# Residual written into product banks by ScalarE, and half of the low parts on VectorE, in two convolution stages

## The reference

```python
# layer 2
out = conv3x3(gn(x), w3 * m3) + einsum('oi,bihw->bohw', w1 * (~m3), gn(x)) + b.sum(axis=1)
x = x + out
# layer 3
g = gn(x)
t = relu(bn(conv3x3(g, w1), ...1))
x = x + relu(bn(conv3x3(t, w2), ...2) + g)
```

## Time and profile before

| what | value |
|---|---|
| median of 3 runs | 3720.85 us (3720.38 to 3724.54) |
| time of the profiled execution | 3722.6 us |
| its span, first to last instruction | 3720.8 us |
| mean granted TensorE clock | 0.977 of full |
| PE busy | 3507.0 us, 94% of the span |
| DVE busy | 2367.6 us, 64% |
| ACT busy | 2116.1 us, 57% |
| POOL busy | 1666.0 us, 45% |

### The profile page before, as it was taken

One profiled execution on the slowest core, in us unless ns is written; L12 is line 12 of the kernel. 1 busy time (PEld: TensorE's weight loads), 2 busy tenths in 40 slices (PEclk: granted clock), 3 DMA queues, 4 the chain that ended last, 5 costly groups with the idle time before them and its releaser, 6 DMA issues. The chain is left out here.

```text
span 3720.8 us, 102442 instructions
## 1 busy us (share of the span) xinstructions
PE 3507.0 (94%) x31974; PEld 2970.3 (80%) x31974; DVE 2367.6 (64%) x6299; ACT 2116.1 (57%) x5882; POOL 1666.0 (45%) x2591
## 2 busy tenths in 40 slices
PE   7999899999999999969999999999999969979999
PEld 4656565656565665569999999999999969979998
DVE  5868787878778787833333333343333359988898
ACT  4979797979788787834443333333333324345554
POOL 2746464646465565600013333333334436556665
PEclk9999999999999999989999999999999979989999
DMA  6232323333232314111110000000002100000000
GB/s 222 69 101 74 99 77 93 83 94 82 85 90 66 101 58 118 48 73 45 51 40 0 0 0 0 0 0 0 0 17 62 62 16 1 1 31 18 35 35 35
DMA packets 202834, 193.93 MB, mean 52 GB/s; under 512 B 35745, under 2 KB 191137, under 8 KB 199457
## 3 DMA queue, kind: packets, MB, share of 16 engines
q1 hardware_dynamic: 171168, 177.15, 15.3%
q10 hardware_dynamic: 31360, 12.87, 1.3%
HBM read 123.30 MB, written 66.58 MB: 51 GB/s over the span
## 5 line engine op out<-in xcount | busy, mean ns | idle before, releaser
L197 PE MATMUL bank<-h,w_hh 128*128 128x128 f32 x8032 | 933.8, 275 | 0.0
L197 PEld LDWEIGHTS bank<-h,w_hh 128*128 128x128 f32 x8032 | 917.0, 192 | 0.0
L242 ACT ACTIVATE h<-bank,bg 128x128 f32<-128x128 f32 x1008 | 370.4, 367 | 818.2 <-PE bank L197 818.1
L1611 ACT ACTIVATE Pr<-bank,nmx 128x256 f32<-128x256 f32 x1568 | 724.0, 479 | 96.5 <-DVE nmx L1749 81.8
L1541 POOL TENSOR_TENSOR Pr<-Pr,rden 128x768 f32<-128x768 f32 x392 | 575.8, 1469 | 379.8 <-DVE rden L1828 379.8
L1749 DVE TENSOR_REDUCE nmx<-bank 128x1 f32<-128x256 f32 x1568 | 555.5, 416 | 173.6 <-PE bank L1955 167.8
L288 DVE SCALAR_TENSOR_TENSOR inp<-bank,b_in,tz 128x256 f32<-128x256 f32 x196 | 85.8, 479 | 696.3 <-ACT tz L225 696.3
L1966 PE MATMUL bank<-ident,Pr 128*128 128x128 f32 x3136 | 463.2, 285 | 17.4 <-POOL Pr L1541 14.8
L1966 PEld LDWEIGHTS bank<-ident,Pr 128*128 128x128 f32 x3136 | 335.4, 142 | 136.2 <-POOL Pr L1541 68.6
L1533 POOL COPY kg<-kT 128x64 f32 x1568 | 309.1, 244 | 296.2 <-DMA row<-ix 276.8
L1620 ACT ACTIVATE PT<-bank 128x512 f32<-128x512 f32 x784 | 427.3, 602 | 24.4 <-PE bank L1966 21.9
(11 more groups left out here) (263 smaller groups left out, 6480.6 us busy)
## 6 DMA issues: line engine op xcount, KB each, us to landing
v_rows<-v_padded SPq DMA_DIRECT2D x168, 232.0 KB, 3.3
vg<-v_windows SPq DMA_DIRECT2D x1176, 32.0 KB, 2.1
first_gates<-gate_sums SPq DMA_DIRECT2D x28, 512.0 KB, 2.6
gate_sums<-first_gates SPq DMA_DIRECT2D x28, 512.0 KB, 3.6
v_padded<-vpad SPq DMA_DIRECT2D x56, 232.0 KB, 2.1
X<-in_x SPq DMA_DIRECT2D x8, 1568.0 KB, 15.6
vg<-v_windows ACTq DMA_DIRECT2D x392, 32.0 KB, 2.2
x_backup<-X SPq DMA_DIRECT2D x8, 1568.0 KB, 6.0
```

What stands on the lines that cost most here:

```text
L197: ins = pe.matmul(bank[m][:, tt * COLS:(tt + 1) * COLS], w_hh[:, k, m * 128:(m + 1) * 128], prev[:, k, :], start=False, stop=(k == NH - 1) ...
L242: act.activation(h[:, 2 * q + tt, m, :], bank[m][:, tt * COLS:(tt + 1) * COLS], ACT.Tanh, bias=bg[:, 0, m:m + 1]).then_inc(s_h, 1)
L1611: act.activation(Pr[:, par, j, :], bank[j][:, 0:KEYS], ACT.Exp, bias=nmx[:, par, j:j + 1], accum_out=den[:, par, j:j + 1])\
```

## The change

In both stages:

- The residual goes into PSUM ahead of the products. A new ACT step `residual(q+1)` writes what is to be added to even columns into the bank of p0, and the negative of what is to be added to odd columns into the bank of p3 (two instructions of 128x392, function Identity with a bias; in the pair, for `i` = 1 only, also with a scale). The matmuls of these two banks (`held`) add onto it: their first one no longer starts a new sum.
- The outputs of every block are the four instructions that the pair's first convolution has already: ACT copies p1 (`first(q)`), DVE forms e = p2 + o, o = o - p2, e = e + p0, and later o = o - p3. L828, L829, L832 and L834 of the masked convolution become two, as do L1076, L1077, L1080 and L1082 of the pair. The pair's L999 (128x784 on ACT) is gone.
- The low part of the first half stays on POOL. That of the second half moves to DVE as `rest_lo(q)`, one instruction of 128x896 with both inputs in SBUF. In DVE's order it stands behind `outputs(q-2)`; in the masked convolution `part_stats(q-3)` follows it.

Once: PE runs four 128x512 float32 matmuls into banks 0, 3, 4 and 7 ahead of the masked convolution, DVE forms the negatives `nbsum`, `nA` and `ntb`, and the blocks 0 and 1 of each stage get their `rest_lo` ahead of the loop.

```diff
-def split_product(pe, ps, w, x, first, last):
+def split_product(pe, ps, w, x, first, last, held=False):
-    pe.matmul(ps, w[0], x[0], start=first, stop=False)
+    pe.matmul(ps, w[0], x[0], start=first, stop=False, skip_group_check=held)
...
                 def lo(q):
-                    for h in range(2):
-                        pool.wait_ge(s_hi, 2 * q + h + 1)
-                        pool.tensor_tensor(halves(v[:, q % 3, 1], h), halves(pts, h),
-                                           halves(v[:, q % 3, 0], h).bitcast(F32), ALU.subtract).then_inc(s_lo, 1)
+                    pool.wait_ge(s_hi, 2 * q + 1)
+                    pool.tensor_tensor(halves(v[:, q % 3, 1], 0), halves(pts, 0),
+                                       halves(v[:, q % 3, 0], 0).bitcast(F32), ALU.subtract).then_inc(s_lo, 1)
...
+                def residual(q):
+                    x = xrows(q).rearrange("p (k e) -> p k e", e=2)
+                    if q >= 2:
+                        act.wait_ge(s_e, 4 * (q - 1))
+                    act.activation(bank[4 * (q % 2)][:, 0:PROD], x[:, :, 0], ACT.Identity, bias=bsum[:]).then_inc(s_res, 1)
+                    act.activation(bank[4 * (q % 2) + 3][:, 0:PROD], x[:, :, 1], ACT.Identity, bias=nbsum[:], scale=-1.0)\
+                        .then_inc(s_res, 1)
+
+                def first(q):
+                    act.wait_ge(s_res, 2 * q + 2)
+                    act.wait_ge(s_m, 4 * q + 1)
+                    act.activation(xrows(q).rearrange("p (k e) -> p k e", e=2)[:, :, 1],
+                                   bank[4 * (q % 2) + 1][:, 0:PROD], ACT.Copy).then_inc(s_s1, 1)
...
                 for q in range(NQ):
                     n, b = divmod(q, NRB)
+                    first(q)
+                    if q + 1 < NQ:
+                        residual(q + 1)
                     if q + 2 < NQ:
                         hi(q + 2)
...
+                def rest_lo(q):
+                    dve.wait_ge(s_hi, 2 * q + 2)
+                    dve.tensor_tensor(halves(v[:, q % 3, 1], 1), halves(pts, 1),
+                                      halves(v[:, q % 3, 0], 1).bitcast(F32), ALU.subtract).then_inc(s_lor, 1)
+
                 def outputs(q):
-                    dve.wait_ge(s_m, 4 * q + 1)
-                    dve.scalar_tensor_tensor(o_, ps[1], bsum[:], o_, ALU.add, ALU.add).then_inc(s_e, 1)
-                    dve.scalar_tensor_tensor(e, ps[1], bsum[:], e, ALU.add, ALU.add).then_inc(s_e, 1)
+                    dve.wait_ge(s_s1, q + 1)
                     dve.wait_ge(s_m, 4 * q + 2)
-                    dve.wait_ge(s_e, 6 * q + 1)
+                    dve.tensor_tensor(e, ps[2], o_, ALU.add).then_inc(s_e, 1)
                     dve.scalar_tensor_tensor(o_, ps[2], -1.0, o_, ALU.mult, ALU.add).then_inc(s_e, 1)
-                    dve.wait_ge(s_e, 6 * q + 2)
-                    dve.tensor_tensor(e, ps[2], e, ALU.add).then_inc(s_e, 1)
...
                     if q + 2 < NQ:
                         points(q + 2)
                     outputs(q)
+                    if q + 2 < NQ:
+                        rest_lo(q + 2)
                     if q:
                         part_stats(q - 1)
...
+                pe.wait_ge(s_gd, GN_DVE + 5)
+                for j in (0, 3, 4, 7):
+                    pe.matmul(bank[j][:], group4[:], X[:, 0:512], start=True, stop=True).then_inc(s_own, 1)
                 pe.wait_ge(s_u, SPLIT_STEPS)
                 for q in range(NQ):
-                    pe.wait_ge(s_lo, 2 * q + 2)
+                    pe.wait_ge(s_lo, q + 1)
+                    pe.wait_ge(s_lor, q + 1)
                     if q >= 2:
-                        pe.wait_ge(s_e, 6 * (q - 1))
+                        pe.wait_ge(s_e, 4 * (q - 1))
                     for j in ORDER:
+                        held = j in (0, 3)
+                        if held:
+                            pe.wait_ge(s_res, 2 * q + (1 if j == 0 else 2))
```

More of the change, by code:

```diff
@@ L657, in _ @@
                         again_tensor(pe, r * PM + PA, r * PM + PM, r * PM + PM, r * 3 + 9)
-def split_product(pe, ps, w, x, first, last):
-    pe.matmul(ps, w[0], x[0], start=first, stop=False)
-    pe.matmul(ps, w[0], x[1], start=False, stop=False)
-    return pe.matmul(ps, w[1], x[0], start=False, stop=last)
+def split_product(pe, ps, w, x, first, last, held=False):
+    pe.matmul(ps, w[0], x[0], start=first, stop=False, skip_group_check=held)
+    pe.matmul(ps, w[0], x[1], start=False, stop=False, skip_group_check=held)
+    return pe.matmul(ps, w[1], x[0], start=False, stop=last, skip_group_check=held)
 BORDERS = 4
@@ L721, in masked_conv @@
         b2 = sb("b2", [C, C])
-        bsum = sb("bsum", [C, 1])
+        bsum, nbsum = sb("bsum", [C, 1]), sb("minus_bsum", [C, 1])
         u_hi, u_lo = sb("u_hi", [C, 12, C], F32R), sb("u_lo", [C, 12, C], F32R)
@@ L787, in _ @@
                 hi(1)
+                act.wait_ge(s_wr, 5)
+                act.wait_ge(s_own, 4)
+                residual(0)
                 for q in range(NQ):
                     n, b = divmod(q, NRB)
+                    first(q)
+                    if q + 1 < NQ:
+                        residual(q + 1)
                     if q + 2 < NQ:
@@ L803, in _ @@
                 dve.tensor_reduce(bsum[:], b2[:], AXX, ALU.add).then_inc(s_wr, 1)
-                dve.wait_ge(s_wr, 3)
+                dve.wait_ge(s_wr, 4)
+                dve.tensor_scalar(nbsum[:], bsum[:], -1.0, None, ALU.mult).then_inc(s_wr, 1)
                 def points(q):
@@ L857, in _ @@
                 points(0)
+                rest_lo(0)
                 points(1)
+                rest_lo(1)
                 for q in range(NQ):
@@ L882, in _ @@
                             ins = split_product(pe, bank[4 * (q % 2) + j][:, 0:PROD], (u_hi[:, k, :], u_lo[:, k, :]),
-                                                (v[:, q % 3, 0, SLOT[j], at], v[:, q % 3, 1, SLOT[j], at]), dy == 0, dy == 2)
+                                                (v[:, q % 3, 0, SLOT[j], at], v[:, q % 3, 1, SLOT[j], at]),
+                                                dy == 0 and not held, dy == 2, held)
                         ins.then_inc(s_m, 1)
@@ L928, in formed @@
         def formed(q):
-            n, i, b = block_of(q)
-            return n * 10 * NRB + (4 * NRB + 6 * b if i else 4 * b)
+            return 4 * q
         def halves(t, h):
@@ L996, in first, with residual @@
                         act.wait_ge(s_f, nth(q - 2) + 1)
+                    act.wait_ge(s_m, 4 * q + 1)
+                    act.activation(yp[q % 2][:, :, 1], bank[4 * (q % 2) + 1][:, 0:PROD], ACT.Copy).then_inc(s_s1, 1)
+                def residual(q):
                     n, i, b = block_of(q)
                     if i:
[L999 to L1003, removed]
+                        x = xrows(n, b).rearrange("p (k e) -> p k e", e=2)
+                        act.wait_ge(s_e, formed(q - 1))
+                        act.activation(bank[4 * (q % 2)][:, 0:PROD], x[:, :, 0], ACT.Identity,
+                                       bias=tb[:, n:n + 1], scale=A[:, n:n + 1]).then_inc(s_res, 1)
+                        act.activation(bank[4 * (q % 2) + 3][:, 0:PROD], x[:, :, 1], ACT.Identity,
+                                       bias=ntb[:, n:n + 1], scale=nA[:, n:n + 1]).then_inc(s_res, 1)
                 def finish(q):
@@ L1020, in _ @@
                 hi(1)
-                act.wait_ge(s_k, 10)
+                act.wait_ge(s_k, 12)
                 for q in range(NQ):
@@ L1073, in outputs @@
                     dve.wait_ge(s_s1, q + 1)
[L1074 to L1086, removed]
+                    dve.wait_ge(s_m, 4 * q + 2)
+                    dve.tensor_tensor(e, ps[2], o_, ALU.add).then_inc(s_e, 1)
+                    dve.scalar_tensor_tensor(o_, ps[2], -1.0, o_, ALU.mult, ALU.add).then_inc(s_e, 1)
                     dve.wait_ge(s_m, 4 * q + 3)
@@ L1138, in _ @@
                     for j in ORDER:
+                        held = i == 1 and j in (0, 3)
+                        if held:
+                            pe.wait_ge(s_res, 2 * nth(q) + (1 if j == 0 else 2))
                         for dy in range(3):
```

31 lines of the change are left out of this document (22 added, 9 removed).

## The result

| | before | changed |
|---|---|---|
| median of 20 runs each | 3718.78 us (3712.20 to 3724.54) | 3726.18 us (3722.93 to 3733.83) |
| span of the profiled execution | 3720.8 us | 3723.2 us |

The ratio is 1.0021, 95% interval 1.0014 to 1.0027: slower by 0.14 to 0.27%, 5 to 10 us; the medians lie 7.4 us apart. Forecast were 3726.7 us and +5.9 us.

The account below looks back on a forecast made before the run. PE was taken to bound the masked convolution at 6.40 us a block, with DVE's turn setting the pace after the change. Masked +6.6 us and pair -0.7 gave +5.9 on 3720.8: 3726.7 us, range 3716 to 3736.

Parts of the forecast that it names:

- PE bound in the masked convolution: Masked convolution: PE busy 99.96 of 100 us, 6.40 us a block; relieving DVE or POOL shortens only the stage's ends.
- the hold: Both stages: rest_lo on DVE stands still while POOL subtracts, ending 0.87 us after POOL.
- rival A: Both stages: no hold, rest_lo shares with POOL without waiting; masked -1.3 us, time 3695 us; chance 0.12.
- Masked turn 6.68: Masked convolution: points, hi, lo, rest_lo and part_stats in series make DVE's turn 6.68 us against 6.38.
- Residual hidden in the masked convolution: Masked convolution, ACT: two residual writes of 0.60 us end their issue at 1.59, before hi at 1.72; no cost.
- rival B: ACT between L843 and hi: dear residual delays hi if two issues exceed 1.13 us; 3733 to 3747 us; chance 0.25.
- Pair: Pair: turns of 6.77, 5.99, 6.95 and 7.21 us, image 54.44 against 54.51, stage -0.7 us.
- PE's busy share 93 to 96: Masked convolution: PE's busy share in 3100:3200 falls to about 93 to 96.
- The four float32 matmuls: Start of the masked convolution: 3.7 us, 7.4 at half clock, within PE's 16.2 us wait; cost 0.
- C: Both stages: the change does not reach the bound, masked within 3 us and pair -8, 3715 us; chance 0.11.
- D: PE: gaps let its clock fall; decides only if most blocks run at half clock, over 3800 us; chance 0.02.
- the line at 0.2%: Whole kernel: change within 0.2%, 7.4 us, can't be told from none; chance 0.47 inside, 0.38 over 3728.3 us.

Follow-up runs that it names:

- stats_first: Changed kernel, but in the masked convolution DVE does part_stats(q-1) ahead of rest_lo(q+2); 3716.95 us, 0.9989 of the kernel before.
- pool_short: Changed kernel, but POOL's subtraction in the masked convolution covers 448 elements instead of 896, zeros for the rest; 3714.67 us, 0.9983 of the kernel before.
- residual_thrice: Changed kernel, but the masked convolution's first residual write is done twice, three writes a block; 3745.10 us, 1.0076 of the kernel before.
- both_moved: Changed kernel with part_stats ahead of rest_lo in the masked convolution, and the pair's rest_lo moved into the next turn; 3694.01 us, 0.9935 of the kernel before.
- hi_first: Changed kernel, but ACT does hi(q+2) ahead of residual(q+1) in both stages; 3723.01 us, 1.0011 of the kernel before.

## Why the prediction was right

- **PE bound in the masked convolution, nothing to gain there but at the ends.** Right in the main: when the hold was gone (stats_first) the stage came 3.3 us below the one before, where rival A's term was -1.3. About 1.2 of it are no end but the middle, where DVE's average of 6.56 us a turn had begun to hold PE up in the kernel before.
- **The hold, 0.87 after POOL's end.** Shown by stats_first and pool_short. `rest_lo` measured 1.80 against 1.78, and 1.07 to 1.08 when free against 1.09.
- **Masked turn 6.68.** Measured 6.70; stage +6.7 against +6.6. That the sum is so close is in part luck: the start gave back 2.0 where 1.4 was forecast and the 28 turns cost 9.0 where 8.4 was, and the two misses cancel.
- **Residual hidden in the masked convolution.** Right, but with nothing to spare. `residual` took 0.62 against 0.60, and from its start to hi the two issues took 1.13 us (3111.66 to 3112.79), which is exactly where rival B begins; the forecast had 1.00. residual_thrice shows what it costs beyond that point. B's price of 3747 for issues of 1 us does not follow from its own terms: with 0.90 to the next issue the masked turns cost 28 x 0.67 and the pair's 14 x 0.58 more, which gives about 3754.
- **Pair: turns of 6.77 with L1147, 5.99 on `z_pad`, 6.95 and, with a residual, 7.21 on `mid_pad`, image 54.44.** Measured, from L1141 to L1141: 6.76 to 6.79, 5.95 to 6.01, 6.96 or 6.97, 7.21 to 7.25, and 54.46. Stage -0.5 against -0.7. L1147 fell to 0.976 in the mean, as forecast, and what it gave up went into L1121's 1.71. L840, the former L816, is 0.61 in the mean, as forecast.
- **PE's busy share 93 to 96.** Missed by the figure named: 96.99. By matmuls (528 of 563) it is 94%, so the gaps were as forecast, and the busy share understates them.
- **The four float32 matmuls, 0.** They took 6.0 us (3.7 to 7.4 forecast) between the group norm and the first product, and behind them PE waited 8.7 us more for `rest_lo`.
- **The rule of the Trainium skill that spoke against the change** ("SBUF — State Buffer", Who interferes with whom) holds here: 1.80 against 1.07 for one instruction with two SBUF inputs. That it is a read port that the two share, no run here shows apart from other ways in which POOL's instruction could hold DVE's. The other rule of the Trainium skill ("ScalarE: Activation LUTs", Step-by-step: what each stage is for, just behind the section that the prediction names) shows no gain here. L1045 writes PSUM in 0.703. L1597 (0.756 for 448 elements) and L999 of the kernel before (1.029 for 784), the same function writing SBUF, lie 0.81 ns an element apart, which gives 0.71 for 392, an estimate.
- **Rival A** did not occur, but it named nearly the right prize, 26 us under the kernel before: with the hold avoided, not absent, both_moved came to 24.6 under it. **C** and **D** did not occur; the granted clock stayed 1.00 in the windows of both stages.
- **The chances.** The forecast of +0.16% had 0.47 inside the line at 0.2% and 0.38 beyond it. The measured +0.21% lies 0.4 us beyond; by the stages alone, +6.2 us, it is inside. That a change under 0.2% can't be told from none was wrong: the interval, 0.14 to 0.27%, is clear of zero.

## What to carry to other kernels

Moving half of one engine's load to another gained nothing here, where the two then stood in one chain: hi, POOL's half, DVE's half and the next turn's points became serial, and each kept the others waiting. Before such a move, list for every instruction with two SBUF inputs on DVE what POOL is doing at that moment, and put PSUM or one-input work (outputs, statistics) beside POOL and the two-input work where POOL is idle; the order alone was worth 32 us here (0.9935 against 1.0021 of the kernel before). And a busy share near 1 can be a wait: compare the mean of a group with the same shape elsewhere in the trace.

## What the runs showed of the hardware that I had not expected

- Executions of the same early work differ by several us: the copy into `gn_gm` ahead of the masked convolution began between 3019.17 and 3026.43 us in eleven profiled executions whose code up to there is the same. Most of it arises in the attention stage: the first copy into `gn_gm`, at that stage's end, began between 1581.6 and 1587.3, and from it to the next the executions differ by 1.5 us only. Why is open. The pair's length in seven of them with the old placement of `rest_lo` or the old pair lay within 0.92 us (460.56 to 461.48, hi_first aside). A change in late stages is better read from marks in the trace than from the total.
- ScalarE's time for 128x392 grew with its operands: into PSUM it took 0.62 us with a bias per channel (L788) and 0.70 with a bias and a scale per channel (L1045). A Copy out of PSUM into SBUF took 0.506; it differs in function, source and place at once, so which of them makes it shorter is not shown.
